# A fused decoder layer on one core: one tanh for the four LSTM gates, four-row matmul operands padded to 128 rows, self-attention weights from small ScalarE activations

## The reference, cut to what matters

```python
pw = _lstm(layernorm(x), W_ih, W_hh, b_ih, b_hh)           # 56 steps, 20 units, gates i f g o
#   c = sigmoid(f) * c + sigmoid(i) * tanh(g);  h = sigmoid(o) * tanh(c)
mu_w = relu(pw @ W_mu.T + b_mu); sigma = sigmoid(pw @ W_sig.T + b_sig)
mu[j] = mu_w[j,0] * mu[j-1] + mu_w[j,1] / s + mu_w[j,2] * (j + 1) / s
w = exp(-(i / (j + 1) - mu[j]) ** 2 / (2 * sigma[j] ** 2)) where i <= j, else 0
x1 = x + (w / norm(w)) @ layernorm(x)
x2 = x1 + cross_attention(layernorm(x1), ctx)              # softmax over 1500 rows, 16 heads, + bO
n = layernorm(x2); e = argmax(n @ W_router)
y = gelu(n @ W1[e] + b1[e]) @ Wo + bo + n;  out = x2 + layernorm(y) * gamma + beta
```

## Time and profile before

| what | value |
|---|---|
| median of the runs | 1596.07 us (3 runs, 1593.94 to 1597.94) |
| the profiled execution's own time | 1587.43 us |
| its span, first to last instruction | 1585.7 us |
| mean granted TensorE clock | 0.985 |
| PE busy, share of the span | 96% |
| DVE, ACT, POOL busy | 71%, 57%, 50% |

### The profile page before, as it was taken

How to read it: one execution, slowest core, us unless ns; L and a number is a source line. 1 busy time by engine, 2 the same in 40 slices (tenths; PEclk the granted TensorE clock), 3 DMA queues, 4 the chain that set the end, 5 groups by cost and what they waited for, 6 DMA issues and landing times.

```text
span 1585.7 us, 25257 instructions
## 1 busy us (share of the span) xinstructions
PE 1517.7 (96%) x7555; PEld 1084.1 (68%) x7555; DVE 1131.3 (71%) x1872; ACT 903.5 (57%) x1283; POOL 792.8 (50%) x406
## 2 busy tenths in 40 slices
PE   6886899999999999999999999999999999999997
PEld 3345667777777777777777777777777777776674
DVE  4338786868686868686877778686868686868555
ACT  4335675666666666666666666666666566555311
POOL 2003365555555555656565655555555555545511
PEclk9997999999999999999999999999999999999899
DMA  4100011000000000000000000000000000100000
GB/s 157 32 0 20 1 39 40 40 39 39 32 38 28 39 28 38 30 39 39 39 39 39 39 39 39 39 39 39 39 39 39 39 39 39 40 14 7 1 1 24
DMA packets 15059, 54.92 MB, mean 35 GB/s; under 512 B 919, under 2 KB 6122, under 8 KB 15022
## 3 DMA queue, kind: packets, MB, share of 16 engines
q1 hardware_dynamic: 15022, 54.46, 9.0%
HBM read 53.54 MB, written 0.92 MB: 34 GB/s over the span
## 4 chain that ended last, share of the span: by engine, by line
PE 83%; DVE 8%; ACT 5%; issue 3%; DMA 0%; DVEq 0%; POOL 0%; POOLq 0%; ACTq 0%
PE ps L725 34%; PE ps L691 27%; PE ps L597 4%; PE ps L592 3%; PE ps L583 3%; PE ps L784 3%; DVE arena L1282 3%; PE ps L576 2%; ACT arena L982 2%; PE ps L705 2%; PE ps L512 1%; PE ps L713 1%; ACT arena L881 1%; ACT arena L884 1%; DVE arena L1268 1%
## 5 line engine op out<-in xcount | busy, mean ns | idle before, releaser
L1268 DVE TENSOR_TENSOR arena<-arena,ps 125x896 f32<-125x896 f32 x336 | 364.4, 1084 | 96.3 <-PE ps L691 96.0
L449 POOL TENSOR_TENSOR arena<-arena,ring 125x896 f32<-125x896 f32 x192 | 417.6, 2175 | 17.5 <-POOL arena L449 0.5
L691 PE MATMUL ps<-q_hi,ctxT_hi 128*125 128x448 f32 x768 | 400.0, 521 | 4.7 <-ACT arena L976 3.2
L449 POOL TENSOR_TENSOR arena<-arena 125x896 f32<-125x896 f32 x112 | 236.9, 2115 | 307.9 <-ACT arena L982 299.2
L725 PE MATMUL ps<-ring,ctx_nat 125*128 125x448 f32 x768 | 343.0, 543 | 0.0
L976 ACT ACTIVATE ring<-ps 125x896 f32<-125x896 f32 x192 | 176.5, 919 | 237.3 <-PE ps L725 149.1
L691 PE MATMUL ps<-q_hi,ctxT_lo 128*125 128x448 f32 x768 | 281.4, 366 | 0.0
L691 PE MATMUL ps<-q_lo,ctxT_hi 128*125 128x448 f32 x768 | 281.4, 366 | 0.0
L725 PE MATMUL ps<-arena,ctx_nat 125*128 125x448 f32 x576 | 242.9, 544 | 2.4
L1282 DVE TENSOR_TENSOR ring<-ring,ps 125x896 f32<-125x896 f32 x192 | 202.4, 1084 | 0.0
L691 PEld LDWEIGHTS ps<-q_hi,ctxT_hi 128*125 128x125 f32 x768 | 143.9, 187 | 66.6 <-issue 47.3
(11 more groups left out here) (201 smaller groups left out, 1879.7 us busy)
## 6 DMA issues: line engine op xcount, KB each, us to landing
ctx_raw<-in_ctx_dram SPq DMA_DIRECT2D x32, 750.0 KB
ctx_nat<-in_ctx_dram SPq DMA_DIRECT2D x32, 750.0 KB
w_sb<-in_L_ffn_W_dram SPq DMA_DIRECT2D x1, 1024.0 KB
resid<-in_x_dram SPq DMA_DIRECT2D x1, 896.0 KB, 6.0
out_dram<-ctx_raw SPq DMA_DIRECT2D x4, 224.0 KB, 2.5
ctx_raw<-in_L_xattn_WQ_dram SPq DMA_DIRECT2D x1, 512.0 KB
w_sb<-in_L_xattn_WK_dram SPq DMA_DIRECT2D x1, 512.0 KB
w_sb<-in_L_xattn_WV_dram SPq DMA_DIRECT2D x1, 512.0 KB
```

The lines of the kernel that those rows point to most:

```text
L449: g.tensor_tensor(summed, chunk[0] if j == 1 else summed, chunk[j], ALU.add).then_inc(s["prob_added"], 1)
L691: m = mm(score_ps[j % 2][:, half, :], cx[k][:, rows], q[k][:, cols], start=(n == 0), stop=(n == 2))
L1268: v.tensor_tensor(run_max, kept(k, 0) if j == 1 else run_max, score_ps[j % 2], ALU.max).then_inc(s["maxed"], 1)
```

## The change

The LSTM's three sigmoid gates become tanh: weights for i, f and o are halved as they are copied (sigmoid(z) is (1 + tanh(z/2)) / 2), one activation of 20 x 128 replaces two, and DVE takes the halves into three `scalar_tensor_tensor` instructions in place of four `tensor_tensor`. The biases are loaded as columns ahead of the transposes. `pick_e`, `b1_r` and `onehotT` get 128 rows, of which all but four are zero; the zeros are written by ACT in the second period. The self-attention weights' square takes -mu as bias and the exponential takes the scale as a value per row, tile by tile (112 x 112), so DVE's subtraction and multiplication fall away; masks and sums of squares move into DVE's loop over groups of the second layer norm. bO is added in two halves behind POOL's sums of the first two periods. PE gets 12 unneeded matmuls around the weights' stage.

```diff
-        pick_e = sb("pick_e", [E, E, 128], F32R)
+        pick_e = sb("pick_e", [128, E, 128], F32R)
-        b1_r = sb("b1_r", [E, 2, FF], F32R)
-        onehotT = [sb(f"onehotT{q}", [E, GT], F32R)[:] for q in range(GROUPS)]
+        b1_r = sb("b1_r", [128, 2, FF], F32R)
+        onehotT = [sb(f"onehotT{q}", [128, GT], F32R)[:] for q in range(GROUPS)]
...
+            for column, bias in ((PE, b_ih), (PE + 1, b_hh)):
+                sp.dma_start(w_hh_in[0:4 * PE, column:column + 1], bias.rearrange("(n a) -> n a", a=1)).then_inc(s["lstm_w_in"], 16)
...
                 g.tensor_tensor(wsum[:, tiles], wsum[:, tiles], minus_half[:, tiles], ALU.pow).then_inc(s["norm_done"], 1)
-            for q in range(GROUPS):
                 power(2, q)
-            need(pool, "ln_done", 2 * GROUPS)
-            g.tensor_tensor(resid_k, resid_k, bO_b[:, None, :].to_broadcast((TOK, PAIRS, D)), ALU.add).then_inc(s["bO_added"], 1)
...
+                if isinstance(i, int) and i == 0:
+                    tiles = slice(k * PAIRS // 2, (k + 1) * PAIRS // 2)
+                    if k == 0:
+                        need(pool, "ln_done", 2 * GROUPS)
+                    g.tensor_tensor(resid_k[:, tiles, :], resid_k[:, tiles, :], bO_b[:, None, :].to_broadcast((TOK, PAIRS // 2, D)), ALU.add).then_inc(s["bO_added"], 1)
...
+            def keep_busy(count, bank):
+                for n in range(count):
+                    mm(ps[:, bank, 0:WARM], ident[:], qk_w[:, 0:WARM // D, :].rearrange("p h d -> p (h d)"), start=True, stop=True)
+            need(pe, "folded_sb", H)
+            need(pe, "ctxT_lo_done", 2 * MP - 1)
+            keep_busy(2, SIDE)
             pe.wait_ge(s["rows_picked"], 1)
...
+            keep_busy(5, SIDE)
             def turn_gauss(q):
...
+            keep_busy(5, SIDE)
             turn_tokens(TOKEN_BANKS[1], 2, 0)
...
-                    a(gate_act[:, 0:3, :], gates[:, 0:3, :], ACT.Sigmoid).then_inc(s["sig_ready"], 1)
-                    a(gate_act[:, 3, :], gates[:, 3, :], ACT.Tanh).then_inc(s["tanhg_ready"], 1)
-                    need(act, "cell_step", 3 * t + 3)
-                    a(cell_t, cell, ACT.Tanh).then_inc(s["tanhc_ready"], 1)
+                    a(gate_act[:, 0:4, :], gates, ACT.Tanh).then_inc(s["tanhg_ready"], 1)
+                    need(act, "cell_step", 2 * t + 2)
+                    a(cell_t, cell, ACT.Tanh, scale=0.5).then_inc(s["tanhc_ready"], 1)
...
+            def gauss_weights(q):
+                if q == 0:
+                    act.wait_ge(s["mu_ready"], 1)
+                for t in range(G4 * q, G4 * q + G4):
+                    m = a(gauss_d[:, t, :], rel, ACT.Square, bias=mu_tok[:, 0, t:t + 1])
+                m.then_inc(s["gauss_sq"], 1)
+                act.wait_ge(s["gauss_sq"], q + 1)
+                for t in range(G4 * q, G4 * q + G4):
+                    m = a(gauss_w[:, t, :], gauss_d[:, t, :], ACT.Exp, scale=mu_tok[:, 1, t:t + 1])
+                m.then_inc(s["gauss_exp"], 1)
...
+            for n in range(GROUPS + 1):
                 if n < GROUPS:
+                    gauss_weights(n)
+                if n:
+                    gauss_weight_square(n - 1)
+                    copy_gauss(n - 1)
...
+            def zero_pads():
+                for n in range(2):
+                    a(b1_r[:, n, :].rearrange("p (m c) -> p m c", m=MB), ident[:, None, :].to_broadcast((128, MB, 128)), ACT.Copy, scale=0.0).then_inc(s["pads_zeroed"], 1)
+                for q in range(GROUPS):
+                    a(onehotT[q].rearrange("p (m c) -> p m c", m=G4), ident[:, None, 0:TOK].to_broadcast((128, G4, TOK)), ACT.Copy, scale=0.0).then_inc(s["pads_zeroed"], 1)
+                act.wait_ge(s["pads_zeroed"], 2 + GROUPS)
...
+                    if isinstance(i, int) and i == 0 and k == 1 and j == 9:
+                        zero_pads()
...
-                    need(dve, "sig_ready", t + 1)
-                    need(dve, "cell_step", 3 * t)
-                    v.tensor_tensor(cell_f, gate_act[:, 1, :], cell, ALU.mult).then_inc(s["cell_step"], 1)
+                    need(dve, "cell_step", 2 * t)
                     need(dve, "tanhg_ready", t + 1)
-                    v.tensor_tensor(cell_i, gate_act[:, 0, :], gate_act[:, 3, :], ALU.mult).then_inc(s["cell_step"], 1)
-                    need(dve, "cell_step", 3 * t + 2)
-                    v.tensor_tensor(cell, cell_f, cell_i, ALU.add).then_inc(s["cell_step"], 1)
+                    v.scalar_tensor_tensor(cell_parts, gate_act[:, 0:2, :], 1.0, gate_act[:, 3:5, :], ALU.add, ALU.mult).then_inc(s["cell_step"], 1)
+                    need(dve, "cell_step", 2 * t + 1)
+                    v.scalar_tensor_tensor(cell, cell_parts[:, 1, :], 0.5, cell_parts[:, 0, :], ALU.mult, ALU.add).then_inc(s["cell_step"], 1)
...
             dve.wait_ge(s["causal_made"], 3)
-            for n in range(GROUPS + 3):
...
+            gauss_mask(0)
             def add_self_attention(q):
+                if q + 1 < GROUPS:
+                    gauss_mask(q + 1)
+                gauss_norm(q)
                 dve.wait_ge(s["norm_done"], q + 1)
```

More of the change, by code:

```diff
@@ L449, in period @@
                     g.tensor_tensor(summed, chunk[0] if j == 1 else summed, chunk[j], ALU.add).then_inc(s["prob_added"], 1)
-                    if isinstance(i, int) and i == PAIRS - 2 and k == 0 and j in POWERS_AT:
-                        power(3, POWERS_AT.index(j))
+                if isinstance(i, int) and i == 0:
[3 more added lines that the diff above has]
+                    g.tensor_tensor(resid_k[:, tiles, :], resid_k[:, tiles, :], bO_b[:, None, :].to_broadcast((TOK, PAIRS // 2, D)), ALU.add).then_inc(s["bO_added"], 1)
+                if isinstance(i, int) and i == PAIRS - 2 and k == 0:
+                    for q in range(GROUPS - 1):
+                        power(3, q)
             sequence(pool, period)
@@ L866, in _ @@
             need(act, "zeros_made", 3)
-            a(cell_t, cell, ACT.Sigmoid).then_inc(s["table_loaded"], 1)
+            a(cell_t, cell, ACT.Tanh).then_inc(s["table_loaded"], 1)
             act.wait_ge(s["lstm_w_ps"], 1)
             need(act, "biased_cleared", 2)
-            a(wihT, ps[:, 3, 0:4 * PE], ACT.Copy).then_inc(s["lstm_w_sb"], 1)
-            a(whhT[0:PE, :], ps[0:PE, 3, 128:128 + 4 * PE], ACT.Copy).then_inc(s["lstm_w_sb"], 1)
-            a(headT[0:PE, :], ps[0:PE, 3, 256:256 + NB + 1], ACT.Copy).then_inc(s["lstm_w_sb"], 1)
+            for start, stop, half in ((0, 2 * PE, 0.5), (2 * PE, 3 * PE, 1.0), (3 * PE, 4 * PE, 0.5)):
+                a(wihT[:, start:stop], ps[:, 3, start:stop], ACT.Copy, scale=half).then_inc(s["lstm_w_sb"], 1)
+                a(whhT[0:PE + 2, start:stop], ps[0:PE + 2, 3, 128 + start:128 + stop], ACT.Copy, scale=half / 2).then_inc(s["lstm_w_sb"], 1)
+            a(headT[0:PE + 1, :], ps[0:PE + 1, 3, 256:256 + NB + 1], ACT.Copy, scale=0.5).then_inc(s["lstm_w_sb"], 1)
             for q in range(GROUPS):
@@ L1017, in copy_onehot @@
                 need(act, "onehotT_ps", q + 1)
-                a(onehotT[q], ps[0:E, bank, 0:GT], ACT.Copy).then_inc(s["onehotT_sb"], 1)
+                a(onehotT[q][0:E], ps[0:E, bank, 0:GT], ACT.Copy).then_inc(s["onehotT_sb"], 1)
+            def zero_pads():
[4 more added lines that the diff above has]
+                act.wait_ge(s["pads_zeroed"], 2 + GROUPS)
             def side_copies(i, k, j, places):
@@ L1201, in _ @@
             v.tensor_copy(bO_b[:], ps[0:TOK, 3, 128:128 + D]).then_inc(s["picks_read"], 1)
-            then(v.tensor_copy(mu_tok.rearrange("p a k -> p (a k)"), ps[0:TOK, 3, 0:2 * PAIRS]))
+            v.tensor_scalar(mu_tok.rearrange("p a k -> p (a k)"), ps[0:TOK, 3, 0:2 * PAIRS], -1.0, None, ALU.mult).then_inc(s["mu_ready"], 1)
             def tiles(q):
@@ L1302, in add_heads @@
                     need(dve, "recip_done", 4 * (pair + 1))
+                    need(dve, "bO_added", 2)
                 for n in range(4):
@@ L1413, in _ @@
                 run_maximum(0, 0, j)
-            need(dve, "bO_added", 1)
             def period(i, k):
```

81 lines of the change are left out of this document (23 added, 58 removed).

## The result

The changed kernel takes 1580.9 us (median of 4 runs, 1578.74 to 1583.72) against 1596.11 us (4 runs): a ratio of 0.9911, 95% interval 0.9888 to 0.9933. The forecast was 1583. Run again later, beside 15 runs of the kernel before, it took 1582.74 against 1589.85, a ratio of 0.9938 (0.9915 to 0.9960). So it is faster, by some 7 to 15 us.

A forecast was written before the change was run, and what follows sets the result against it. PE was taken to bound most of the span, DVE the weights stage. Terms -5.2 + 6.3 - 2.5 + 0.2 + 1.0 - 7.9 - 4.8 = -12.9 took 1587.4 to 1574.5 in the trace; with runs 8.6 higher, 1583.2, range 1575 to 1592.

The forecast's parts named there:

- A: Likeliest case, 0.54: whole kernel, all terms come as forecast, 1583 us, its own range 1579 to 1587.
- C: Rival, 0.18: in the experts, half clock from the new wait for POOL on, 2.6 us less gain, 1585.8 us.
- Weights stage: Self-attention weights, `mu_tok` to first score: eight DVE instructions go but the order becomes serial, +6.3 us (bounds +4.5, +8.5).
- (a): Weights stage start: four squares, table load, four exponentials, then the next group's eight activations and mask, 5.2 us.
- (b): Weights stage, group 0: PE's transposes and product at half clock, then addition and moments, 5.65 us.
- (c): Weights stage, group 1: group 2's mask, transposes and product, addition and moments, scaling of the earlier group, 7.35 us.
- (d): Weights stage, group 2: PE back at full clock, 1.8 instead of 3.1 us for its part, 6.1 us in all.
- (e): Weights stage, group 3: no mask; sum and POOL 2.0, addition and moments 2.56, two scalings 2.2, together 6.75 us.
- (f): Weights stage end: transpose, copy and hops, 1.25 us.
- B: Rival, 0.12: the handoff between PE's matmuls is not about rows, padding gives nothing, nor does the clock; 1596 us, the same.
- E: Rival, 0.05: the new wait for POOL leaves PE at half clock for the rest of the experts; slower, 1606 us.
- D: Rival, 0.11: the weights stage takes its upper bound and the LSTM its lower, +2.2 + 3.6, 1589 us.

## Why the prediction was right, point by point

The forecast time was met, 1583 against 1580.9, and so was its sign. But the sum made on the trace was not: 1574.5 was to come for the traced execution, 1583.7 came. Two errors, of 9.2 us in the sum and 11.4 in the step from trace to runs, cancelled but for 2. That the number was met so well is luck; what held is the sign and most of the mechanisms. Of the signs that were to show it, the step of 1.71, the gap of 1 us and the spacing of the blocks came; the first score 32.8 behind `mu_tok` (34.7 came) and an end without half clock behind 1486 us did not. What came is A with C's half clock.

**LSTM.** The step was right to the hundredth (1.71), hop and 128-column tanh included. The term was 1.45 too large in the trace: "The 16 steps written out have no register instruction and I give them nothing" is where it failed, since the last eight lost 1.15, most of it at half clock. The other 0.3 is a first step that starts later (21.16 us against 20.85).

**Weights stage.** The mechanism was right, the size 2.2 short. Followed by the steps of the sum, from the end of `mu_tok`'s copy at 126.06: (a) 6.8 instead of 5.2, because four small activations overlap less than I took (0.31 apart, 1.22 in all); (b) 5.5, (c) 7.1, nearly as put; (d) 7.1 instead of 6.1, because PE was not back at full clock (half until 149.3); (e) 6.8 and (f) 1.3, as put. That DVE waits for a product which PE's order puts behind the next group's transposes was in (b) and (c); the run with the order turned showed it.

**bO.** 2.5 forecast, 2.3 in the trace. The later halves cost nothing that the trace shows. The move of POOL's powers has no term in the sum; with the half clock that stood there before only, it is the -3.4 of the table.

**Zeros.** The stall was right (0.95 for 1.0). The term was 5.9 all the same, past its bound of 3: I priced the wait and not the clock behind it, though I had done so for the wait in the experts.

**Padding, groups 1 to 3.** -8.6 for -7.9. The rule of the Trainium skill that I weighed ("TensorE: Matmul & The Clock Gate", section "Why this matters for your kernels") holds here for a single matmul's duration (at full clock in the kernel before, 0.36 to 0.47 with four rows and with 128) and not for the starts: 0.37 us a block came back. The run with 32 rows and its loads show that it is the change of row count between neighbours that costs.

**Padding, group 0.** -2.3 for -4.8: the blocks ran at full clock and the wait came, as forecast, and then rival C's half clock: 2.2 was my price for that case.

**The step that failed** is the last one: "the runs lie 8.6 higher, so 1596.07 becomes 1583.2". It carried the gap between runs and trace over to the changed kernel. That gap is for the most part half clock in the experts, among the four-row blocks (7.5 of 9.2 us between the two traces of before; before's runs are long where their granted clock is low), and padding takes it away: the changed kernel's traced execution lies 2.8 us above its median. So padding was worth more than its term in the runs (15.1 alone), and zeros, stage, group 0 and LSTM cost more than theirs, together 4.9 + 2.2 + 2.5 + 1.45 = 11 us in the trace (less 0.7 for the larger padding term and 1.3 for -3.4 and +2.1 in the later periods: the 9.2, but for rounding). Rivals B and E are refuted by the padding run, C's half clock came (its time, 1585.8, did not), and D came half true (the LSTM short of its term and the stage at its upper bound).

## What to carry to other kernels

Give neighbouring matmuls on a busy PE the same row count (here 128, that of the others), and read their cost from starts, not durations. Time each part of a change alone, and look whether a part's run holds a second edit. Before ACT or another engine gets extra work in the middle of a PE stream, price a short PE stall with the half clock that may follow it, and put the work where PE doesn't wait. A median of runs above a traced execution is not a constant to be carried over: ask which stretch makes the difference and whether the change touches it.

## What the runs showed of the hardware that was not expected

A stall of 0.95 us ahead of a block of sums was followed by 10.2 us at half clock in four traces out of four, and the same sums without the stall by none in ten. PE's weight load was not pulled ahead between matmuls of 32 and 128 rows (0.31 us of idle loader), nor between 4 and 128, but was 0.2 us ahead within a pair of equal rows. Sums of one column each ran at half clock behind a wait of 0.51 us as behind one of 2.62. A DVE subtraction of two SBUF operands, 1.09 us alone, took 4.32 beside a POOL addition, and which of two such subtractions is hit made PE's wait 3.22 or 4.98 us.
